# The ends of a round's experts in one load, and the loop over rounds rotated by half a chunk

## What is computed

```python
x = x + attention(layernorm(x), ctx, ctx)
h = layernorm(x).reshape(-1, 256)
shared_out = (silu(h @ shared_gate) * (h @ shared_up)) @ shared_down
logits = h @ gate_w
topk_ids, topk_val = argmax(logits), max(logits)          # one of 32 experts per token
xs = h * sigmoid(topk_val)
sorted_x = xs[argsort(topk_ids)]
g = ragged_dot(sorted_x, routed_gate_w, tokens_per_expert)
u = ragged_dot(sorted_x, routed_up_w, tokens_per_expert)
d = ragged_dot(silu(g) * u, routed_down_w, tokens_per_expert)
return x + shared_out + d[inverse of the sort]
```

## Time and profile before

| | us |
|---|---|
| timed runs | 306.15, 307.87, 311.05 |
| their median | 307.87 |
| the profiled execution, its own time | 305.98 |
| its span, first to last instruction | 304.2 |
| TensorE's matmuls busy in the span | 261.5 (86%) |
| VectorE busy | 155.4 (51%) |
| ScalarE busy | 93.7 (31%) |
| GpSimd busy | 88.0 (29%) |

### The profile page before, as it was taken

How to read it: one execution, slowest core, us unless ns; L and a number is a source line. 1 busy time by engine, 2 the same in 40 slices (tenths; PEclk the granted TensorE clock), 3 DMA queues, 4 the chain that set the end, 5 groups by cost and what they waited for, 6 DMA issues and landing times.

```text
span 304.2 us, 12929 instructions
## 1 busy us (share of the span) xinstructions
PE 261.5 (86%) x4628; PEld 183.6 (60%) x4629; DVE 155.4 (51%) x490; ACT 93.7 (31%) x284; POOL 88.0 (29%) x248
## 2 busy tenths in 40 slices
PE   4978999998798999979889999899899899889710
PEld 3736656653473488657667777677677677643600
DVE  0547877884599321145454555455455455423423
ACT  2056766542311102243232333233233233212000
POOL 1245121111017764022222222222222222202772
PEclk9996899999999999999999999999999999999995
DMA  6999994000002235209989599999999999524575
GB/s 197 343 371 374 375 372 147 0 3 2 0 0 95 103 99 188 69 4 321 321 291 312 155 317 301 367 386 385 371 375 382 384 371 373 186 48 110 165 207 163
DMA packets 53039, 68.69 MB, mean 226 GB/s; under 512 B 3966, under 2 KB 35099, under 8 KB 53019
## 3 DMA queue, kind: packets, MB, share of 16 engines
q1 hardware_dynamic: 46203, 61.60, 58.9%
q0 software_dynamic: 1536, 4.20, 4.5%
q10 hardware_dynamic: 5280, 2.62, 3.3%
HBM read 59.49 MB, written 8.91 MB: 225 GB/s over the span
## 4 chain that ended last, share of the span: by engine, by line
PE 70%; DVE 8%; issue 7%; POOL 5%; DMA 4%; ACT 4%; POOLq 1%; ACTq 1%; SPq 1%; DVEq 0%
PE bank L1016 26%; PE bank L1038 15%; PE bank L941 13%; PE bank L953 5%; POOL xs_flat L462 4%; PE bank L872 3%; PE bank L907 2%; DMA slot_rows<-late 2%; DVE h_place L530 1%; PE bank L890 1%; DVE h_place L531 1%; DMA bq_row<-in_L_xattn_bias_q_dram 1%; ACT h_place L740 1%; DMA xs_flat<-slot_rows,slot_i 1%; PE bank L845 1%
## 5 line engine op out<-in xcount | busy, mean ns | idle before, releaser
L1016 PE MATMUL bank<-ring_gu,x_c 128*32 128x128 f32 x2528 | 86.5, 275 | 7.9 <-issue 5.9
L1016 PEld LDWEIGHTS bank<-ring_gu,x_c 128*32 128x32 f32 x2528 | 65.9, 109 | 23.3 <-issue 20.5
L1038 PE MATMUL bank<-ring_d,h_place 128*32 128x128 f32 x1264 | 51.0, 276 | 4.4 <-DVE late L653 1.0
L455 POOL COPY x_c<-xs_flat 128x32 f32 x79 | 16.6, 210 | 99.1 <-PE bank L1016 86.6
L1038 PEld LDWEIGHTS bank<-ring_d,h_place 128*32 128x32 f32 x1264 | 32.2, 108 | 19.3 <-issue 17.1
L643 DVE TENSOR_TENSOR h_place<-h_place,bank 128x128 f32<-128x128 f32 x79 | 22.7, 288 | 40.2 <-ACT h_place L775 40.2
L780 ACT COPY late<-bank 64x128 f32 (+1 forms) x79 | 20.5, 259 | 51.9 <-PE bank L1038 51.9
L775 ACT ACTIVATE h_place<-bank 128x128 f32<-128x128 f32 x79 | 21.9, 278 | 44.0 <-PE bank L1016 44.0
L647 DVE STREAM_TRANSPOSE h_place<-h_place 128x128 f32<-128x128 f32 x79 | 24.6, 311 | 14.4 <-PE bank L1038 9.8
L953 PE MATMUL bank<-shd,h_place 128*128 128x256 f32 x128 | 28.4, 380 | 2.1 <-DVE h_place L531 2.1
L653 DVE TENSOR_TENSOR late<-bank,late 64x128 f32 x79 | 23.1, 293 | 13.8 <-ACT late L780 12.5
(11 more groups left out here) (133 smaller groups left out, 255.7 us busy)
## 6 DMA issues: line engine op xcount, KB each, us to landing
ring_gu<-L_ffn_routed_gate_w_dram SPq DMA_DIRECT2D x32, 512.0 KB, 8.5
ring_gu<-n_L_ffn_routed_up_w_dram SPq DMA_DIRECT2D x32, 512.0 KB, 9.5
ring_d<-L_ffn_routed_down_w_dram SPq DMA_DIRECT2D x32, 512.0 KB, 9.9
slot_rows<-late ACTq DMA_DIRECT2D x10, 256.0 KB, 5.8
x<-in_x_dram SPq DMA_DIRECT2D x4, 512.0 KB, 6.8
slot_rows<-zeros SPq DMA_DIRECT2D x1, 2048.0 KB, 14.4
late<-sorted_rows SPq DMA_DIRECT2D x8, 256.0 KB, 3.3
out_dram<-x SPq DMA_DIRECT2D x8, 256.0 KB, 2.4
```

Of the source, the lines that this page charges most:

```text
L455: g_.tensor_copy(x_c[:, 0], xsT[:, 0, bass.ds(col, LW)]).then_inc(x0_part, 1)
L1016: ins = te.matmul(bank[g][q * LW:(q + 1) * LW, 0:P].rearrange("p (m f) -> p m f", f=LW), x_c[:, k], columns[:, q], start=(k == 0), stop=(k ...
L1038: ins = te.matmul(bank[2][r:r + LW, 0:DH], hT[:, f * LW:(f + 1) * LW], ring_d[:, s, f, a * DH:(a + 1) * DH], start=(m == 0), stop=(m == HA ...
```

## The change

One table, turn, takes the place of turn_first and turn_end. It has 33 values: a 1, and behind it the end of each expert plus one; so value e is the first chunk of expert e, and value e + 1 its end. VectorE writes it with a memset and one operation.

TensorE reads seven values of it at the head of a round (the first chunk of the round's first expert, and six ends) with one load, and three values ahead of the two experts that are left over. No expert reads its own end any more. The round is rotated: the gate and up products of the very first chunk stand ahead of the loop. In the loop each expert first runs its other chunks (other_chunks), then the gate and up products of the first chunk of the next expert and behind them its own last down product (next_expert). The last of the six calls goes to slot 0 of the next round. The branch on the round's number is gone.

```diff
--- before.py
+++ after.py
@@ -186,8 +186,7 @@
         done_before = sb("done_before", [P, NE])
         begin_f = sb("begin_f", [P, 1])
         begin = sb("begin", [1, P], I32)
-        turn_first = sb("turn_first", [1, NE], I32)
-        turn_end = sb("turn_end", [1, NE], I32)
+        turn = sb("turn", [1, NE + 1], I32)
         block_n = sb("block_n", [1, 1], I32)
         chunk_end = sb("chunk_end", [1, NE], I32)
 
@@ -620,9 +619,8 @@
             step(v.tensor_scalar(block_n[:], chunk_cum[0:1, NE - 1:NE], -1.0, None, ALU.add))
             step(v.tensor_scalar(block_n[:], block_n[:], STORE.bit_length() - 1, None, ALU.arith_shift_right))
             v.tensor_copy(chunk_end[:], chunk_cum[0:1]).then_inc(table_ready, 1)
-            v.tensor_scalar(turn_end[:], chunk_cum[0:1], 1.0, None, ALU.add).then_inc(table_ready, 1)
-            v.scalar_tensor_tensor(out=turn_first[:], in0=chunk_cum[0:1], scalar=1.0, in1=chunk_f[0:1],
-                                   op0=ALU.add, op1=ALU.subtract).then_inc(table_ready, 1)
+            v.memset(turn[:, 0:1], 1).then_inc(table_ready, 1)
+            v.tensor_scalar(turn[:, 1:NE + 1], chunk_cum[0:1], 1.0, None, ALU.add).then_inc(table_ready, 1)
 
 
             shared_residual(0)
@@ -1042,31 +1040,39 @@
 
             n_chunks = chunk_count(pe)
 
-            def expert(w, e, s, before, landed):
-
-                pe.wait_ge(gu_in[s], 2 * landed)
-                gate_up(w, s)
-                end = pe.value_load(turn_end[0:1, bass.ds(e, 1)], min_val=2, max_val=MAX_CHUNKS + 1)
-                if before is None:
-                    with pe.If(it > 0):
-                        down_of(w, RING - 1)
-                else:
-                    down_of(w, before)
+            def turns(e, n):
+                _, values = nc.values_load_multi_w_load_instructions(
+                    turn[0:1, bass.ds(e, n)], engines=(mybir.EngineType.PE,), min_val=1, max_val=MAX_CHUNKS + 1)
+                return values
+
+            def other_chunks(w, end, s, landed):
+
                 pe.wait_ge(d_in[s], landed)
                 with pe.If(w + 1 < end):
                     with pe.Fori(w + 1, end) as more:
                         gate_up(more, s)
                         down_of(more, s)
                     pe.nop()
-                return end
-
+
+            def next_expert(end, s, landed):
+
+                n = (s + 1) % RING
+                pe.wait_ge(gu_in[n], 2 * landed)
+                gate_up(end, n)
+                down_of(end, s)
+
+            pe.wait_ge(gu_in[0], 32)
+            gate_up(1, 0)
             with pe.Fori(0, ROUNDS) as it:
-                w = pe.value_load(turn_first[0:1, bass.ds(RING * it, 1)], min_val=1, max_val=MAX_CHUNKS)
+                w = turns(RING * it, RING + 1)
                 for s in range(RING):
-                    w = expert(w, RING * it + s, s, s - 1 if s else None, 16 * it + 16)
-            w = pe.value_load(turn_first[0:1, RING * ROUNDS:RING * ROUNDS + 1], min_val=1, max_val=MAX_CHUNKS)
+                    other_chunks(w[s], w[s + 1], s, 16 * it + 16)
+                    next_expert(w[s + 1], s, 16 * it + (16 if s + 1 < RING else 32))
+            w = turns(RING * ROUNDS, REST + 1)
             for s in range(REST):
-                w = expert(w, RING * ROUNDS + s, s, s - 1 if s else RING - 1, 16 * ROUNDS + 16)
+                other_chunks(w[s], w[s + 1], s, 16 * ROUNDS + 16)
+                if s + 1 < REST:
+                    next_expert(w[s + 1], s, 16 * ROUNDS + 16)
             down_of(n_chunks + 1, REST - 1)
```

## The result

| | before | after |
|---|---|---|
| median, us | 307.01 (306.07 to 311.05, 4 runs) | 328.21 (326.67 to 333.22, 4 runs) |
| the profiled execution | 305.98 | 326.67 |
| its span | 304.2 | 324.9 |
| its mean granted clock | 0.974 | 0.944 |

The changed kernel is slower: 1.0685 of before, 95% interval 1.0611 to 1.0758. The direction was forecast, but the time lies 11.2 us above the forecast and 5.2 us above the range. The ratio, here and in the experiments, leaves out executions in a slower state (311.05 before and 333.22 after); the ranges and medians do not. The two profiled executions, 20.7 us apart, are compared from here on.

What follows compares the result with a forecast made beforehand. TensorE was taken to be bound by a 1.64 us chunk cycle over bank 2, with turns costing more; turns 5.4, last step 0.5, start 0.8, load 4.2, less 1.0, made +9.9 us on 307.0: 317 us, range 310.5 to 323.

Steps and rivals of the forecast that it cites:

- What bounds the kernel: Inside an expert, down product, copy, addition and next down product share single bank 2: 1.64 us a chunk; weights in time.
- Going under 1.64 at a change: Sign of being wrong: changes of expert inside a round get shorter than the 1.64 us cycle.
- all single loads together: Inside rounds, 26 single loads of turn_end at changes of expert leave the path at 0.04 us each: 1.0 us off.
- The turn: Last down product of a round to first of the next: 4.35 us instead of 2.91, flat load; 5.4 us on.
- The last step: Step to the last two experts, loading three values: 3.0 us against 2.45, 0.5 us on.
- the start (0.8): Start of the loop, seven-value load behind the first chunk: 3.4 us to the second gate product, 0.8 us on.
- the low end: Lower bound of the range: flat load on the fastest execution, 1 us off for errors of the gaps, 310.5 us.
- The load: Multi-value load at turns, start and last step: 0.13 us per further value, 32 values, 4.2 us, bounds 0 to 8.3.
- The rival of the flat load: Seven values load in 0.31 us like one, leaving 5.7 us on, 312 to 313 us; chance 0.19.
- the clock: Rival: idle TensorE at turns falls to half clock, up to 3 us a turn, 325 to 332 us; chance 0.09.
- A clock under 1.00 in the loop: Sign of being wrong: the granted clock, forecast at 1.00 through the loop, is under 1.00 there.
- The sequencer ahead: Rival: at turns the sequencer loads and checks while TensorE's queue holds work; 7.3 us won, 299.7 us; chance 0.05.

Runs made afterwards that it cites:

- with filled gaps: Changed kernel plus idle-bank matmuls of 512 columns after each round's last down product: six a round 329.4 us, ratio 1.0655; four 322.91 us, ratio 1.0471.
- the second kernel with moved code: Changed kernel with 32 matmuls behind a never-taken branch ahead of the routed loop, 130 instructions more: 330.06 us, ratio 1.0785.
- the kernel with the load alone: Kernel before, its order and branch kept and without the rotation, but with table turn and the load of seven values: 321.25 us, ratio 1.0388.
- that edit alone: Kernel before with a round's first chunk number carried over the turn in a register, not loaded: 303.92 us, ratio 0.9877.

## Why the prediction was wrong

**What bounds the kernel** was read rightly, for the later rounds. From the second round on the cycle of 1.64 us holds inside an expert in all kernels, at changes of expert it is now 1.64 to 1.70 too away from the turns, and no wait for weights appears in the changed kernel. In the first round it is no floor: chunks take 1.55 to 1.76 us there before and 1.55 to 1.69 after, at full clock and apart from the stop, and one change of expert that took 1.76 (143.48 to 145.24) now takes 1.55 (146.48 to 148.03). Going under 1.64 at a change was named as a sign of being wrong. It touches a few tenths of a microsecond: all single loads together gave 0.8 us and not 1.0.

**The turn** was summed rightly: 4.35 us with a load of 0.31. With the measured load it gives 4.35 + 0.77 = 5.12 for turn 4, which took 5.14; for turn 1, 5.77 against 5.83; for turns 2 and 3, less the half clock, 5.13 and 5.75 against 5.2 and 5.8. The last step was 0.15 us shorter than its sum, and the start (0.8) was as said. One bound was added up a little wrong: the low end by its own terms is 305.98 + 5.7 - 1 = 310.7, not 310.5.

**The load** was mis-sized: 4.2 us forecast, 5.6 measured, since 0.13 us a value holds only for the loads that begin on a multiple of four values; the other two and that of three values pay 0.235. That is inside the bounds given (0 to 8.3), and only 1.4 us. The Trainium skill (Runtime: NRT & Kernel Launch, section Instruction fetch mechanics) gives about 200 ns a register, for loads from HBM. These loads read SBUF: a further value costs 235 ns in the dear ones and 130 in the others, above and below that figure. The rival of the flat load (0.19) is dead: no load of seven was under 1.07 us.

**The step that failed is the clock.** The prediction had the mechanism as a rival, with 3.9 us without a weight load at a turn (measured 3.94 to 4.61) and up to 3 us for each, and gave it 0.09. It argued that 1.62 us without a weight load before had left the clock at 1.00. That row excludes nothing: it shows a gap well under half of the one to come. The gap of 3.9 us was longer than any in the loop of before, and the only evidence on a thin stretch, rows 9, showed a fall. The clock fell behind all five long gaps, that of the start too, and cost 7.6 us, 1.5 a gap; only 1 us of it was in the range. A clock under 1.00 in the loop was one of the prediction's own signs of being wrong. The right form was to add it to the sum and not to set it beside it: with the 1.5 us measured since, 307.0 + 9.9 + 5 x 1.5 gives 324.4. Without the half clock the measured 328.2 would be 320.6, inside the range. The price of up to 3 us a turn was for 6.8 us at half clock; in this profile four of the five falls lasted 3.4, and 6.8 stood at turn 2 alone. The Trainium skill (TensorE: Matmul & The Clock Gate, section What's actually happening) says that an idle TensorE is given half its clock; the trace agrees, with 0.50 behind gaps of 3.49 to 4.61 us, and the runs without assertions and with filled gaps show it by its absence.

**A term was missing:** the stop in the first passage through the loop's code, 1.4 us longer here than before, and some 4 us longer in the second kernel with moved code (2.60 + 5.81 against one cycle and 2.82). The stop stood in the trace of before (148.66, 0.94 us of "issue" in mid-product), and is in none of the rows that the prediction used.

**The sequencer ahead** (0.05) did not happen at a turn. At the start it does: in the kernel with the load alone it ran at 127.0, while TensorE still had work queued.

## What to carry to other kernels

Reading values together saves the starts of the loads, but it puts their whole price in one place. Ask whether that place has cover: here 26 loads that cost 0.8 us in all, and the small ones at the turns, were exchanged for six large ones with nothing beside them, and the seven bounds assertions, 2.0 us, cost more than the reading, 1.1 to 1.7. Where an instruction stream makes TensorE stand still for as long as it did here (3.5 to 4.6 us), add the half clock behind it to the sum. The cheapest value is the one already in a register: that edit alone gave 1.2% (0.5 to 2.0).

## What was new about the hardware

- A load of several values from SBUF into registers costs 0.31 us for one, 0.78 for three, and for seven 1.09 if the first stands on a multiple of four values in this table's tile, else 1.72; moving the table by two values exchanged the prices.
- Asserting one loaded value costs 0.146 + 0.018 us and two gaps, 0.28 in all, on the engine's own sequencer.
- The length of a gap alone does not decide whether the clock falls. In the routed loop and at its start, over all profiles, it fell in or behind every gap of 3.94 us or more but one (3.97 us at turn 4 of the second kernel with moved code, 265.04 to 269.01, where it stayed at 1.00), behind all six of 3.46 to 3.59 at the start, and behind one of two of 3.76. It did not fall behind a stop of 3.27 (seven single loads, first round), yet it did at 155.05 behind one of 2.41 (table moved by two values), and at 133.35 in the kernel with the load alone, where no gap was over 1.83. Each of these falls lasted 3.4 or 6.8 us.
- The first run through this loop's code stops for 0.8 to 4.1 us, each time ending 2.3 to 3.4 us behind the start of a 16 KB packet of the instruction queue, and where depends on where the code lies; later rounds have neither such a stop nor such a packet.
